# The scan stage of a two-layer kernel: the loop over groups becomes seven passes of straight code

## The reference, cut to what matters

```
proj = h @ in_proj_w.T                       # gate, hBC, dt
hBC  = silu(causal_conv(hBC))                # 4 taps; hid, B, C
M    = (C @ B.T) * exp(segsum(A * dt))       # in chunks of 128 tokens
y    = M @ (hid * dt) + C @ carried_states + Dp * hid
yg   = y * silu(gate)
y    = yg * rsqrt(mean(yg * yg) over the group)
out  = x + y @ out_proj_w.T
```

## Time and profile before

| | us |
|---|---|
| median of 3 runs | 2113.58 |
| the runs | 2108.7, 2113.58, 2115.81 |
| the profiled execution | 2109.39 |
| its span, first to last instruction | 2107.4 |
| PE busy in it | 1978.7 (94%) |
| DVE, ACT, POOL busy | 1604.0, 1472.5, 1224.7 |

### The profile page before, as it was taken

One profiled execution on the slowest core, in us unless ns is written; L12 is line 12 of the kernel. 1 busy time (PEld: TensorE's weight loads), 2 busy tenths in 40 slices (PEclk: granted clock), 3 DMA queues, 4 the chain that ended last, 5 costly groups with the idle time before them and its releaser, 6 DMA issues.

```text
span 2107.4 us, 36786 instructions
## 1 busy us (share of the span) xinstructions
PE 1978.7 (94%) x10874; PEld 1581.9 (75%) x10874; DVE 1604.0 (76%) x3002; ACT 1472.5 (70%) x2946; POOL 1224.7 (58%) x848
## 2 busy tenths in 40 slices
PE   6987688988999999999999999999999999999986
PEld 5563566667788887888788878887888888788875
DVE  8557787965778786877777778877787778778777
ACT  4242676645778787777777787777787778778774
POOL 5524465753466666556565666665665565566655
PEclk9999799999999999999999999999999999999999
DMA  4604323244333333333243333333333333332433
GB/s 177 196 24 129 107 80 112 84 140 135 118 119 119 105 115 111 108 106 126 91 137 101 126 100 128 126 101 115 110 117 117 111 114 117 98 126 90 137 113 120
DMA packets 114364, 242.41 MB, mean 115 GB/s; under 512 B 23665, under 2 KB 24689, under 8 KB 113522
## 3 DMA queue, kind: packets, MB, share of 16 engines
q1 hardware_dynamic: 110322, 227.32, 32.9%
q0 software_dynamic: 3840, 12.59, 2.0%
HBM read 227.01 MB, written 12.85 MB: 114 GB/s over the span
## 4 chain that ended last, share of the span: by engine, by line
PE 73%; issue 1%; DVE 1%; ACT 1%; DMA 0%; SPq 0%; DVEq 0%; ACTq 0%
PE s_ps L71 13%; PE s_ps L73 12%; PE s_ps L72 12%; PE s_ps L1708 6%; PE s_ps_o L73 5%; PE s_ps_o L71 5%; PE s_ps_o L72 5%; PE s_ps L1678 5%; PE s_ps L1716 4%; PE s_ps L1670 3%; PE s_ps L1698 1%; PE s_ps L1656 1%; ACT s_lm L1788 0%; DMA s_wo_raw<-in_w_out 0%; PE s_ps L1662 0%
## 5 line engine op out<-in xcount | busy, mean ns | idle before, releaser
L2090 POOL TENSOR_TENSOR w_lo<-w_raw,w_hi 128x1024 fp32r<-128x1024 f32 x142 | 339.8, 2398 | 572.9 <-ACT w_hi L1770 572.9
L71 PE MATMUL s_ps<-h_hi,w_hi 128*128 128x512 f32 x1152 | 463.0, 402 | 9.2 <-DVE s_hid L1939 6.1
L73 PE MATMUL s_ps<-h_hi,w_lo 128*128 128x512 f32 x1152 | 450.7, 391 | 0.0
L72 PE MATMUL s_ps<-h_lo,w_hi 128*128 128x512 f32 x1152 | 449.9, 391 | 0.0
L1934 DVE SCALAR_TENSOR_TENSOR s_cv<-s_ps,s_par,s_cv 128x511 f32<-128x511 f32 (+2 forms) x480 | 355.8, 744 | 18.8 <-ACT s_cv L1813 12.9
L2107 POOL TENSOR_TENSOR s_lm<-s_lm,s_cbt 128x512 f32<-128x512 f32 x256 | 325.8, 1295 | 12.5 <-ACT s_lm L1795 12.5
L1788 ACT ACTIVATE s_lm<-s_rows,s_steps 128x128 f32<-128x128 f32 x1024 | 312.5, 390 | 9.2 <-PE s_ps L1708 9.2
L1813 ACT ACTIVATE s_cv<-s_ps,s_par 128x512 f32<-128x512 f32 x160 | 124.4, 778 | 242.7 <-PE s_ps L73 225.5
L71 PEld LDWEIGHTS s_ps<-h_hi,w_hi 128*128 128x128 f32 x1152 | 217.2, 189 | 54.7 <-DVE s_hid L1939 6.9
L73 PEld LDWEIGHTS s_ps<-h_hi,w_lo 128*128 128x128 f32 x1152 | 217.0, 188 | 46.9
L72 PEld LDWEIGHTS s_ps<-h_lo,w_hi 128*128 128x128 f32 x1152 | 217.7, 189 | 40.8
(11 more groups left out here) (266 smaller groups left out, 4116.5 us busy)
## 6 DMA issues: line engine op xcount, KB each, us to landing
w_raw<-in_w_in SPq DMA_DIRECT2D x144, 512.0 KB, 3.3
s_rows<-acs_dram SPq DMA_DIRECT2D x256, 256.0 KB, 4.4
s_wo_raw<-in_w_out SPq DMA_DIRECT2D x128, 256.0 KB, 3.6
w_raw<-in_gu_q SPq DMA_DIRECT2D x14, 512.0 KB, 3.3
f_d_q<-in_d_q SPq DMA_DIRECT2D x28, 256.0 KB, 2.7
f_d_w<-in_d_s SPq DMA_DIRECT2D x28, 256.0 KB, 3.4
table<-shifted SPq DMA_DIRECT2D x16, 256.0 KB, 3.0
xs<-in_x SPq DMA_DIRECT2D x8, 256.0 KB, 6.2
```

What stands on the lines that cost most here:

```text
L71: nc.tensor.matmul(dst, l_hi, r_hi, start=start, stop=False)
L72: nc.tensor.matmul(dst, l_hi, r_lo, start=False, stop=False)
L73: return nc.tensor.matmul(dst, l_lo, r_hi, start=False, stop=stop)
L2090: nc.gpsimd.tensor_tensor(w_lo[:, slot, :], w_raw[:, slot, :], w_hi[:, slot, :].bitcast(F32), ALU.subtract).then_inc(w_lo_ready, 1)
```

## The change

The loop of the engine becomes a loop of the program that writes the kernel: `g` is now a number, and the two units of a pass stand seven times in the instruction streams of all five engines.

```
             unit(eng, Unit(-1, 1))
             unit(eng, Unit(0, 0, first=True))
-            with eng.Fori(0, GROUPS - 1) as g:
+            for g in range(GROUPS - 1):
                 unit(eng, Unit(g, 1))
                 unit(eng, Unit(g + 1, 0))
             unit(eng, Unit(GROUPS - 1, 1, last=True))
```

## The result

The changed kernel takes 2084.59 us (median of 4 runs, 2082.03 to 2088.05) against 2112.67 for the kernel before (4 runs, 2108.7 to 2115.81): a ratio of 0.9869, with a 95% interval of 0.9846 to 0.9893. 2082 was forecast. The profiled execution took 2086.14 us.

The account below looks back on a forecast made before the run. Prediction: a saturated PE bounds the kernel; the profiled 2109.39 us less 23.2 (jumps) and 5.2 (slots) gives 2081.0, plus 1 us for the rest: 2082 us, 1.5% below 2113.58, range 2076 to 2092.

Parts of the forecast that it names:

- What bounds the kernel: Whole kernel: PE, busy 94% of the span, is saturated in units without a jump; change pays only where PE stops or slows.
- The six jumps, 23.2 us: At the loop's six jumps back: PE idle 13.7 us, the rest lower clock and pipeline refilling; all 23.2 us regained.
- The clock term: Behind three of six jumps PE's clock is at half for a while, making units 1.5 to 3.2 us longer; goes with the gap.
- The slots, 5.2 us: Register and wait instructions between transpose and projection cost PE 0.37 us per unit, 5.2 us in fourteen, regained in straight code.
- The other engines, cost nothing: ACT's stops at jumps and control instructions on DVE, POOL and SP: hidden by PE's saturated stream, so zero gain.
- Length of code, nothing: Fetching the longer straight code on the instruction queues would cost PE zero.
- Rival C: Repeated code must be fetched anew, PE stopping at each piece's end: slower, about 2200 us; chance 0.05.
- rival B: PE's gaps stay, coming wherever code isn't at hand rather than from the jump: 2109 to 2113 us; chance 0.08.
- rival A: Only the jumps pay; the seven slots keep their 85.8 us in straight code: 2087 us; chance 0.18.
- The 1 us for what may come from elsewhere: Added to the sum of 2081.0 us because the profiled run lay 4.2 us below the median of the runs.

Follow-up runs that it names:

- near jumps: The changed kernel with an empty loop of two rounds added on PE at each of the six old pass ends; 2083.71 us.
- Registers without a jump: The changed kernel's straight code, but PE, DVE, ACT and POOL still work their waits out from a register holding zero; 2088.68 us.

## Why the prediction was right, point by point

- **What bounds the kernel.** Right. Straight code runs the units at 97.58 us with PE busy throughout. But "busy for all of it" does not mean that nothing is lost: the loop's units without a jump show it too, and are 0.40 us longer.
- **The six jumps, 23.2 us.** Right in cause and nearly in size: a hint on all engines, which leaves every jump and control instruction in place, takes off 22.6. PE alone straight takes off 22.5, but of that 14 x (97.98 - 97.70) = 3.9 are pace, so some 4.6 us of the 23.2 need the other engines' jumps gone as well. The gap is the fetch of the target's code (hint, near jumps); that it comes twice where the target lies near the end of a block fits the run with the head on a block, whose second stop was gone. The clock term came with the gap: the units of the changed kernel all show 1.00.
- **The slots, 5.2 us.** Right in sum: 97.98 - 97.58 = 0.40 per unit, 5.6 us in fourteen, and the hint, which leaves these instructions in place, leaves 6.2. The step behind it was half wrong. It put the loss down to the instructions that PE's sequencer holds, and read the "issue" of the earlier trace rows as theirs. At the transpose two losses meet: PE's own register instruction, and DVE's state, which comes later while DVE has register instructions too. Either one repaired gives most of the 0.40: PE with all its instructions runs at 97.64 when the other engines are straight, and straight PE at 97.7 when DVE keeps its own. The sum came out because the two stretches of the earlier trace rows differ in both. Registers without a jump show 3.6 of the 5.6 us; what makes the rest isn't shown.
- **The other engines, cost nothing.** Wrong, and not only once PE no longer stops. With PE alone in the loop, where PE stops as before, the units without a jump lose 0.34 us when the other four are straight: PE's busy stream did not hide DVE's late states. With PE straight, the others' loop costs 6.3 us, through DVE's late first result and late states and through ACT. It did not show in the total because the change makes all five straight, and because both terms above were read from units in which all five looped: this cost lies within the 23.2 and the 5.2.
- **Length of code, nothing.** Right: no stop in fourteen units, and fewer packets than before. Rival C is out, and rival B, since there are no gaps; rival A is out, at 85.45 us for seven slots.
- **The 1 us for what may come from elsewhere.** Too small. The stages around the units took 714.4 us in the profile of before (2109.39 - 1394.95), nearly the least of all eleven, and 720.0 in that of after (2086.14 - 1366.13). 1366.1 + 719.3, the mean of the eleven, would be 2085.4; the median is 2084.6. The prediction put much of the 4.2 us between that profile and the median of before down to jumps that lower the clock. The runs of the changed kernel, which has no such jump, spread nearly as far (6.0 us against 7.1), and the part ahead of the first of the fourteen units, the same code in all, took 635.5 to 644.4 us in the eleven profiles. So much of the spread lies outside the units.

## What to carry to other kernels

Where one engine is saturated, cut its loop at equal points and compare a unit with a jump, one behind it and one with none. Idle time at the jump that has no named releaser points to the jump, and the row to look for is a block of equal instructions broken in its middle. If the body has to stay a loop, a prefetch hint for the jump gave back 22.6 of 28.8 us here, and placing the pass's head on a block's first slot 10, half of it idle time and most of the rest the clock. An engine with time to spare can still cost time: here the bound one waited for its result some eighty times, and each was 0.09 us later for the loop. Write the other engines' streams out straight in an experiment, with the bound one as it was, before they are called free. And "issue" can be a wait for another engine that sits on an instruction which the profile doesn't list.

## What the runs showed of the hardware that was not expected

A jump back to code that is at hand costs nothing that can be measured (1366.03 against 1366.13 us with six of them), and one over a whole pass 1.4 to 2.3 us of idle PE on average; the one jump over three passes cost 1.4. PE's fetches are one of the two instruction queues: it moved 89 packets wherever PE was straight and 103 wherever PE looped as before; the other moved 77 with DVE, ACT, POOL and SP straight and 99 with all four in the loop as before. With the hint on the same loops it was 98 and 63. PE's gap at a jump was 2.3 us with all engines jumping and 1.6 us with PE alone; that they fetch at the same time may be the reason, but no run here shows it. The clock fell to half behind three of the six jumps in the first case, and behind five in the second, though the stops were shorter.
